# Projecting V ahead of the norm chain, and one FFN tile's projection inside the weight stage

## The chip, the cores and the metric

The program runs on all 8 NeuronCores of one Trainium2 chip. Each core computes one batch element with the same code and the same weights. There is no traffic between cores. The metric is the device time of the slowest core in microseconds (us).

## The reference, cut to what matters

```
x: (8, 2048, 2048); 16 heads of width 128
a = LayerNorm(x)
q, k, v = a @ W_Q[h] + b_Q, a @ W_K[h] + b_K, a @ W_V[h] + b_V
z = softmax(causal(q k^T / sqrt(128))) v          for each head
x = x + LayerNorm(z @ W_O + b_O)                  W_O summed over heads
bw = where(W >= 0, 1, -1) * mean|W| by row        W: (2048, 2048)
x = x + LayerNorm(LayerNorm(x) @ bw^T + bias)
```

## The kernel before

Every instruction is put by hand into one of five queues (sync, tensor, vector, scalar, gpsimd) by `p.op`. Each queue is executed in the order in which it was written, and what one engine needs of another is a wait on a counter. So where a Python function is called sets the place of its work in all queues at once.

The work of a core has four stages.

1. **LayerNorm 1** (`emit_A_head`, `emit_A_tail`, L235 to L282, loop at L385). The normalised tokens are transposed into `arena_a`, 2048 x 2048 in bf16. The projections of head 0 are done here, four slices of 512 tokens each, as the tokens become ready.
2. **Sixteen heads** (loop at L450). A projection is `emit_w_mms(h, wi)`: 64 matmuls of 128x512 into four PSUM banks, and then four VectorE instructions (L373) that add the bias and move the result to SBUF. `wi` is 0 for Q, 1 for K and 2 for V. Q and V use the banks of `psA` and `psB`, K those of `psD`, `psE` and `psC`. In the vector and tensor queues a head stands in this order: K projection; the norm chain of q (square on VectorE L462, four matmuls with a matrix of ones L471, four maxima L477, one more L483), the same for k, then two logarithms and an exponential on one element (L487 to L503), a matmul that spreads the number over the partitions (`pe_mb`, L507) and its copy to `mbias` (L512); the V projection (L518); the 16 transposes of V (L537) and their copy into `v_sb` (L543); then four groups of query tokens (scores L555, exp L569, causal mask on GpSimd L588 and L591, denominator L601, L606 and L610, scaling L620, product with V L637). The next head's Q projection is put into the tensor queue in the last group, ahead of the product with V (L630). Head 0 has its three projections behind it when the loop starts, so its V transposes stand right behind `pe_mb`.
3. **Weight stage** (`emit_bw_tile`, L398, called 16 times at L667). Each call loads 128 rows of the FFN weight into one of two buffers (`fwst`), takes the sum of absolute values (L411), the sign (L420) and the scaled weight (L423) on VectorE, transposes it on TensorE (L437) into `psD` and `psE`, and copies it to `arena_a` on VectorE (L443).
4. **Output loop** over 16 tiles of 128 tokens (L876). `emit_front_pe(i)` is the output projection: loads of x and z, 64 matmuls (L728) and 4 for the bias (L733) into `psA` and `psB`, two copies to `s1` on ScalarE (L744, L747), the statistics (L759, L762) and the factors (L221, L225, L769). `emit_front_chain(i)` adds the residual (L780) and normalises (L210, L787). `emit_back(i)` is the FFN product and the output. Tile i's projection stands ahead of the back part of tile i-1.

The buffers `xin` (x of a tile) and `s1` lie in memory that attention used and the weight stage does not. `x2` lies where the weight stage's first buffer lies.

Of the kernel before, what the change touches and what calls it, by code (L numbers as in the profile page):

```python
# [60 lines left out]
def build_program(SEQ, DM, H):  # L61
    assert SEQ == DM
    NCH = DM // 128
    NT = SEQ // 128
# [12 lines left out]
    p = Plan(nc)  # L77
# [91 lines left out]
    FWs = [p.sem(f"FW{i}") for i in range(2)]  # L169
# [134 lines left out]

    dv_mbias_d = {}
    dv_bw_evac_half = [0, 0]
# [4 lines left out]
    def emit_w_mms(h, wi, only_slice=None):  # L311
# [15 lines left out]
        for sq0, nq in slices:  # L327
            for c in range(NCH):
                wait = []
                if c == 0:  # L330
# [3 lines left out]
                    if sidx == 0:  # L334
                        prev_evac = dv_qkv_evac_d.get((h, 1), 0) if wi == 2 \
                            else dv_bank_free
                        wait += [("DV", dv_zevac.get(gidx - 1, 0)),
                                 ("DV", dv_mbias_prev),
                                 ("SC", sc_rinv_prev),
                                 ("DV", max(dv_bw_evac_half)),  # L340
                                 ("DV", prev_evac)]
                        if wi == 2:
                            wait.append(("DV", dv_mbias_d.get(h, 0)))
                    else:
                        wait += [("SC", max(psbuf_last_rd)),
                                 ("DV", dv_vch.get(h - 1, 0)),
                                 ("DV", dv_red_last)]
                for k in range(nq):
                    s = sq0 + k
# [100 lines left out]
    for h in range(H):  # L450
        if h > 0:
            emit_w_mms(h, 1)
        dv_mx = [0, 0]
        dv_red_all = {}
        for which, src_sb in ((0, qt_sb), (1, kt_sb)):
            if which == 0:
                w0 = [("DV", dv_qkv_evac_d[(h, 0)]), ("PE", pe_mb_prev),
                      ("PE", pe_bw_last)]
            else:
                w0 = [("PE", pe_norm_last),  # L460
                      ("DV", dv_qkv_evac_d[(h, 1)])]
            dv_sq = p.op("vector", lambda e, s=src_sb: e.tensor_mul(  # L462
                sqb, s[:], s[:]), wait=w0, inc="DV")
            for s in range(NSL):
# [4 lines left out]
                else:  # L469
# [38 lines left out]
            psC[:, 0:1], oner_sb[:], nm_bf[:], start=True, stop=True),  # L508
            wait=[("DV", dv_nm), ("DV", dv_qkv_evac_d[(h, 1)]),
                  ("SC", sc_rinv_prev)], inc="PE")  # L510
# [3 lines left out]
        dv_mbias_prev = dv_mbias  # L514
        dv_mbias_d[h] = dv_mbias

        if h > 0:
            emit_w_mms(h, 2)  # L518
        dv_qkv_evac = [dv_qkv_evac_d[(h, wi)] for wi in range(3)]
        dv_qkv_all = max(dv_qkv_evac)  # L520
        if h + 1 < H:
            for wi in range(3):
                emit_w_load(h + 1, wi)
        wo_start = max(0, H - 4)
        if h >= wo_start:
            win = H - wo_start
            per = (H + win - 1) // win
            hh0 = (h - wo_start) * per
            for hh in range(hh0, min(hh0 + per, H)):
                p.op("gpsimd", lambda e, hh=hh: e.dma_start(  # L530
                    Bz[:, hh * DM:(hh + 1) * DM], wo_h.ap()[hh]),
                    inc="WO", incn=16)

# [127 lines left out]

    B0_PE = p.cnt("PE")
    B0_DV = p.cnt("DV")
    B0_SC = p.cnt("SC")
    B0_GP = p.cnt("GP")
    for t in range(NT):
        emit_bw_tile(t)  # L667

    B_PE = p.cnt("PE")
# [103 lines left out]
    def emit_front_chain(i):  # L773
        nonlocal sc_r3_prev, dv_ln3_prev
        par = i % 2
        wait = [("SC", sc_r2[i]), (XCs[par], xc_t[i])]
        if i == 0:
            wait += [(FWs[0], fw_tot[0]), (FWs[1], fw_tot[1]), ("DV", B_DV)]
        p.drain("vector")
# [12 lines left out]
    def emit_back(i):  # L792
# [51 lines left out]
        for ci, (d, srcp) in enumerate(s2_copies):  # L844
# [29 lines left out]
            wait=[("DV", gp_x3[i])], inc="OUT0", incn=16)  # L874

    for i in range(NT):  # L876
        emit_front_pe(i)
        if i > 0:
            emit_back(i - 1)
        emit_front_chain(i)  # L880
# [53 lines left out]
```

How the kernel before makes its waits and increments, by code:

```python
        def thunk(e, fn=fn, wait=wait, inc=inc, incn=incn, lowp=lowp):  # L43
            for (s, v) in wait:
                e.wait_ge(sems[s][0], v)
            if lowp is not None:
                with nc.allow_low_precision(reason=lowp):
                    ins = fn(e)
            else:
                ins = fn(e)
            if inc is not None:
                ins.then_inc(sems[inc][0], incn)
```

## Time and profile before

| what | value |
|---|---|
| device time, median of 3 runs | 2764.18 us (2762.92 to 2764.88) |
| profiled execution, device time | 2761.78 us |
| its span, first to last instruction, slowest core (core 6) | 2760.0 us |
| spans of the other cores | 2756.1 to 2758.8 us |
| mean granted TensorE clock, all cores | 0.847 to 0.851 of full speed |
| busy: TensorE, VectorE, ScalarE, GpSimd | 71%, 36%, 20%, 9% |
| chain that ended last: TensorE, VectorE, ScalarE, issue | 52%, 18%, 10%, 9% |

The span is the time on which the profile's views are drawn; 1.8 us lie around it. A share of busy time is a mean over four stages with different limits, so a stage is judged by its own stretch of the span. PEclk is the TensorE clock granted, as a fraction of 2.4 GHz: 1.00 is the upper level and 0.50 the lower (1.2 GHz). A row of the timeline reads: start, length, engine, line, operation, what is written and read, how often, and in brackets the idle time ahead of it with what ended it. A length of several instructions is that of the whole row.

### The profile page before, as it was taken

Reading aid. Unit: us, or ns where it says so; the run is one execution under the profiler, and the core shown is the slowest. Engines: PE = TensorE matmul, PEld = TensorE weight load, DVE = VectorE, ACT = ScalarE, POOL = GpSimd, SP = SyncE. Lnnn points to the kernel's source line nnn. Section 1 sums busy time; section 2 is a strip of 40 time slices with the busy share of each in tenths; the row PEclk is TensorE's granted clock in tenths of the full one; section 3 lists DMA queues with packets and bytes.
Section 4 is the critical chain, followed back from the end, with each engine's and each line's share of the span. In section 5 each row is a group of like instructions: output and inputs, shape, how many; then the busy total and the mean of one; then the engine's idle time right before and its main releaser. Section 6 shows DMA issues by size and latency. Waiting matters only on the chain.

```text
span 2760.0 us, 27071 instructions; the slowest of 8 cores (2756.1 to 2760.0 us)
## 1 busy us (share of the span) xinstructions
PE 1956.9 (71%) x8336; PEld 824.0 (30%) x8336; DVE 990.8 (36%) x1760; ACT 554.9 (20%) x737; POOL 239.9 (9%) x558
## 2 busy tenths in 40 slices
PE   2568677677786777867777687677228778778774
PEld 1323232232332323323223232232123333333331
DVE  3532323232322322233223323232772453353353
ACT  1213213123032130321312303123001111111110
POOL 1001101011010110110101111111000000000000
PEclk9679889898898888978989889898559889889887
DMA  6321021120210211102112241320530321221210
GB/s 147 121 24 24 12 27 15 19 29 6 25 24 12 27 14 18 24 12 27 14 19 25 41 56 19 45 37 9 182 107 24 76 77 39 77 77 50 65 54 31
DMA packets 178473, 119.31 MB, mean 43 GB/s; under 512 B 168100, under 2 KB 168100, under 8 KB 170148
## 3 DMA queue, kind: packets, MB, share of 16 engines
q0 software_dynamic: 107200, 75.51, 15.7%
q1 hardware_dynamic: 71140, 42.07, 6.1%
q8 instruction: 78, 1.28, 0.2%
q14 instruction: 55, 0.45, 0.1%
HBM read 125.97 MB, written 25.17 MB: 55 GB/s over the span
## 4 chain that ended last, share of the span: by engine, by line
PE 52%; DVE 18%; ACT 10%; issue 9%; DVEq 5%; POOL 3%; DMA 2%; ACTq 1%; POOLq 0%; SPq 0%
PE psA L359 9%; PE psB L359 9%; PE psE L637 7%; ACT ptil L569 5%; PE psC L824 5%; DVEq L58 4%; PE psC L359 4%; PE psC L601 3%; DVE st L210 3%; PE psD L824 2%; PE psE L824 2%; POOL ptil L591 2%; PE psD L359 2%; PE psE L359 2%; DMA c<-x 2%
## 5 line engine op out<-in xcount | busy, mean ns | idle before, releaser
L620 DVE TENSOR_TENSOR ptil<-ptil,c 128x512 bf16<-128x512 bf16 x640 | 220.3, 418 | 509.0 <-ACT c L610 509.0
L359 PE MATMUL psA<-arena_a,wbuf 128*128 128x512 bf16 x1024 | 323.7, 405 | 10.3 <-DVE mbias L512 6.0
L359 PE MATMUL psB<-arena_a,wbuf 128*128 128x512 bf16 x1024 | 320.1, 401 | 3.2 <-ACT arena_a L276 3.2
L569 ACT ACTIVATE ptil<-psA,mbias 128x1024 bf16<-128x1024 f32 x160 | 178.3, 1114 | 492.7 <-PE psA L555 409.1
L637 PE MATMUL psE<-ptil,v 128*128 128x512 bf16 x640 | 193.5, 399 | 51.3 <-DVE ptil L620 51.3
L601 PE MATMUL psC<-ptil,onem_sb 128*128 128x512 bf16 x640 | 188.8, 411 | 49.9 <-POOL ptil L588 23.2
L824 PE MATMUL psC<-arena_a,c 128*128 128x512 bf16 x512 | 167.2, 411 | 57.5 <-DVE c L811 57.5
L591 POOL TENSOR_TENSOR ptil<-ptil,tri_sb 128x128 bf16<-128x128 bf16 x256 | 109.3, 427 | 1087.9 <-ACT ptil L569 1087.8
L569 ACT ACTIVATE ptil<-psB,mbias 128x1024 bf16<-128x1024 f32 x160 | 177.1, 1107 | 0.2 <-issue 0.2
L555 PE MATMUL psA<-qt,kt 128*128 128x512 bf16 x320 | 112.6, 438 | 75.7 <-ACT ptil L569 48.5
L359 PE MATMUL psC<-arena_a,wbuf 128*128 128x512 bf16 x544 | 157.2, 379 | 4.5 <-DVE qt L373 4.5
L210 DVE BATCH_NORM_STATS2 st<-wbuf 128x6 f32<-128x512 f32 x64 | 39.6, 681 | 313.9 <-ACT wbuf L847 313.9
L359 PEld LDWEIGHTS psB<-arena_a,wbuf 128*128 128x128 bf16 x1024 | 105.5, 103 | 139.7 <-issue 33.4
L359 PEld LDWEIGHTS psA<-arena_a,wbuf 128*128 128x128 bf16 x1024 | 104.3, 102 | 143.2 <-issue 37.7
L555 PE MATMUL psB<-qt,kt 128*128 128x512 bf16 x320 | 113.1, 440 | 22.9 <-ACT ptil L569 22.8
L487 ACT ACTIVATE srow<-srow 1x1 f32<-1x1 f32 x16 | 3.2, 202 | 608.7 <-DVE srow L483 608.7
L637 PEld LDWEIGHTS psE<-ptil,v 128*128 128x128 bf16 x640 | 62.2, 97 | 187.1 <-issue 152.4
L601 PEld LDWEIGHTS psC<-ptil,onem_sb 128*128 128x128 bf16 x640 | 64.8, 101 | 178.2 <-issue 132.0
L471 PE MATMUL psA<-c,onem_sb 128*128 128x512 bf16 x64 | 30.0, 551 | 119.3 <-DVE c L462 119.3
L373 DVE TENSOR_SCALAR ptil<-psA,bqkvT_sb 128x512 bf16<-128x512 f32 x32 | 22.6, 747 | 250.9 <-PE psB L359 245.5
L359 PE MATMUL psD<-arena_a,wbuf 128*128 128x512 bf16 x240 | 90.9, 379 | 21.7 <-DVE c L653 21.7
L824 PE MATMUL psD<-arena_a,c 128*128 128x512 bf16 x256 | 105.4, 412 | 0.0
(121 smaller groups left out, 2269.0 us busy)
## 6 DMA issues: line engine op xcount, KB each, us to landing
c<-fw POOLq DMA_DIRECT2D x16, 1024.0 KB, 5.1
ptil<-x SPq DMA_DIRECT2D x16, 1024.0 KB, 8.2
out<-wbuf POOLq DMA_DIRECT2D x16, 1024.0 KB, 5.5
wbuf<-wq POOLq DMA_DIRECT2D x16, 512.0 KB, 6.6
wbuf<-wk POOLq DMA_DIRECT2D x16, 512.0 KB, 6.7
c<-x SPq DMA_DIRECT2D x8, 1024.0 KB, 5.3
wbuf<-wv POOLq DMA_DIRECT2D x16, 512.0 KB, 6.5
zs<-c SPq DMA_DIRECT2D x64, 128.0 KB, 1.9
```

The source lines that it names most:

```text
L58: self.plans[eng].append(lambda e: e.drain())
L210: p.op("vector", lambda e, g=g, a=src_ap, pr=par: e.bn_stats(st6[pr][:, 6 * g:6 * g + 6], a[:, STW * g:STW * (g + 1)]), wait=w)
L359: e.matmul(banks[bidx], wslot[sl][:, c * 128:(c + 1) * 128], ln1t3[:, c, s * SLW:(s + 1) * SLW], start=(c == 0), stop=(c == NCH - 1)),
L373: e.tensor_scalar(d[:, s * SLW:(s + 1) * SLW], banks[bidx], bqkvT_sb[:, wi * H + h:wi * H + h + 1], None, ALU.add), wait=[("PE", pe_mm)],
L471: pe_norm_last = p.op("tensor", lambda e, s=s, hb=hb: e.matmul([psA[:, 0:SLW], psA[:, 512:512 + SLW], psB[:, 0:SLW], psB[:, 512:512 + SLW] ...
L555: pe_sc[j] = p.op("tensor", lambda e, j=j, g=g, hb=hb: e.matmul(schalf[hb], kt_sb[:, j * 128:(j + 1) * 128], qt_sb[:, g * GQ:(g + 1) * GQ] ...
L569: t_exp = p.op("scalar", lambda e, buf=buf, dst=dst: e.activation(dst, buf, AF.Exp, bias=mbias[:, 0:1], scale=C_ATTN), wait=wait, inc="SC")
L591: gp_mask_j[j] = p.op("gpsimd", lambda e, j=j, r=r: e.tensor_tensor(ptil[:, j * GQ + r * 128:j * GQ + (r + 1) * 128], ptil[:, j * GQ + r * ...
L601: pe_den = p.op("tensor", lambda e, j=j, chunks=chunks: e.matmul(psC[:, 512:512 + GQ], onem_sb[:], pslot[j], start=(j == 0), stop=(j == ch ...
L620: dv_norm[j] = p.op("vector", lambda e, j=j, g=g: e.tensor_tensor(pslot[j], pslot[j], rbc[g % 2], ALU.mult), wait=wait, inc="DV")
L637: pe_av = p.op("tensor", lambda e, j=j, chunks=chunks: e.matmul(psE[:, 0:GQ], v_sb[:, j * 128:(j + 1) * 128], pslot[j], start=(j == 0), st ...
L824: p.op("tensor", lambda e, c=c, s=s: e.matmul(ffnb[s], ln3t[:, c * 128:(c + 1) * 128], bwt3[:, c, s * 512:s * 512 + PSW], start=(c == 0), ...
```

## The change

Two pieces of work are moved, and the waits that go with them.

- For heads 1 to 15 the V projection (`emit_w_mms(h, 2)`) stands right behind the K projection, ahead of the norm chain. It now waits for the copies of Q out of the same banks. The squaring of q waits for the V copies. The loads for the next head and the `wo` loads are written earlier in the text; in the gpsimd queue nothing stands between the two places.
- The weight stage is written behind the definitions of the output loop, and after its fifth tile (t == 4) `emit_front_pe(0)` is called, in all queues: the loads of x and z for token tile 0, its 68 matmuls, the two copies, the statistics and the factors. The output loop then starts with `emit_front_chain(0)`. `emit_front_chain(0)` waits for all loads of the weight stage.

```diff
@@ -302,7 +302,6 @@
     dv_qkv_evac_d = {}
     pe_w_done_d = {}
 
-    dv_mbias_d = {}
     dv_bw_evac_half = [0, 0]
     dv_bw_evac_last = 0
     dv_fw_free = {}
@@ -332,19 +331,17 @@
                     if only_slice is not None:
                         wait.append(("DV", dv_qkv_evac_d.get((h, wi), 0)))
                     if sidx == 0:
-                        prev_evac = dv_qkv_evac_d.get((h, 1), 0) if wi == 2 \
-                            else dv_bank_free
                         wait += [("DV", dv_zevac.get(gidx - 1, 0)),
                                  ("DV", dv_mbias_prev),
                                  ("SC", sc_rinv_prev),
                                  ("DV", max(dv_bw_evac_half)),
-                                 ("DV", prev_evac)]
-                        if wi == 2:
-                            wait.append(("DV", dv_mbias_d.get(h, 0)))
+                                 ("DV", dv_qkv_evac_d.get((h, 0), dv_bank_free))]
                     else:
                         wait += [("SC", max(psbuf_last_rd)),
                                  ("DV", dv_vch.get(h - 1, 0)),
                                  ("DV", dv_red_last)]
+                        if wi == 2:
+                            wait.append(("DV", dv_qkv_evac_d.get((h, 0), 0)))
                 for k in range(nq):
                     s = sq0 + k
                     w = list(wait) if k == 0 else []
@@ -450,15 +447,30 @@
     for h in range(H):
         if h > 0:
             emit_w_mms(h, 1)
+            emit_w_mms(h, 2)
+        dv_qkv_evac = [dv_qkv_evac_d[(h, wi)] for wi in range(3)]
+        dv_qkv_all = max(dv_qkv_evac)
+        if h + 1 < H:
+            for wi in range(3):
+                emit_w_load(h + 1, wi)
+        wo_start = max(0, H - 4)
+        if h >= wo_start:
+            win = H - wo_start
+            per = (H + win - 1) // win
+            hh0 = (h - wo_start) * per
+            for hh in range(hh0, min(hh0 + per, H)):
+                p.op("gpsimd", lambda e, hh=hh: e.dma_start(
+                    Bz[:, hh * DM:(hh + 1) * DM], wo_h.ap()[hh]),
+                    inc="WO", incn=16)
+
         dv_mx = [0, 0]
         dv_red_all = {}
         for which, src_sb in ((0, qt_sb), (1, kt_sb)):
             if which == 0:
-                w0 = [("DV", dv_qkv_evac_d[(h, 0)]), ("PE", pe_mb_prev),
+                w0 = [("DV", dv_qkv_evac[2]), ("PE", pe_mb_prev),
                       ("PE", pe_bw_last)]
             else:
-                w0 = [("PE", pe_norm_last),
-                      ("DV", dv_qkv_evac_d[(h, 1)])]
+                w0 = [("PE", pe_norm_last)]
             dv_sq = p.op("vector", lambda e, s=src_sb: e.tensor_mul(
                 sqb, s[:], s[:]), wait=w0, inc="DV")
             for s in range(NSL):
@@ -506,30 +518,12 @@
             "softmax is shift-invariant so the value need not be exact")
         pe_mb = p.op("tensor", lambda e: e.matmul(
             psC[:, 0:1], oner_sb[:], nm_bf[:], start=True, stop=True),
-            wait=[("DV", dv_nm), ("DV", dv_qkv_evac_d[(h, 1)]),
+            wait=[("DV", dv_nm), ("DV", dv_qkv_evac[1]),
                   ("SC", sc_rinv_prev)], inc="PE")
         pe_mb_prev = pe_mb
         dv_mbias = p.op("vector", lambda e: e.tensor_copy(
             mbias[:], psC[:, 0:1]), wait=[("PE", pe_mb)], inc="DV")
         dv_mbias_prev = dv_mbias
-        dv_mbias_d[h] = dv_mbias
-
-        if h > 0:
-            emit_w_mms(h, 2)
-        dv_qkv_evac = [dv_qkv_evac_d[(h, wi)] for wi in range(3)]
-        dv_qkv_all = max(dv_qkv_evac)
-        if h + 1 < H:
-            for wi in range(3):
-                emit_w_load(h + 1, wi)
-        wo_start = max(0, H - 4)
-        if h >= wo_start:
-            win = H - wo_start
-            per = (H + win - 1) // win
-            hh0 = (h - wo_start) * per
-            for hh in range(hh0, min(hh0 + per, H)):
-                p.op("gpsimd", lambda e, hh=hh: e.dma_start(
-                    Bz[:, hh * DM:(hh + 1) * DM], wo_h.ap()[hh]),
-                    inc="WO", incn=16)
 
         wait = [("DV", dv_qkv_all), ("DV", dv_mx[1])]
         for t in range(NT):
@@ -659,13 +653,6 @@
                 wait=[("DV", dv_zevac[gidx])], inc=ZWs[zpar], incn=16)
             gidx += 1
 
-    B0_PE = p.cnt("PE")
-    B0_DV = p.cnt("DV")
-    B0_SC = p.cnt("SC")
-    B0_GP = p.cnt("GP")
-    for t in range(NT):
-        emit_bw_tile(t)
-
     B_PE = p.cnt("PE")
     B_DV = p.cnt("DV")
     B_SC = p.cnt("SC")
@@ -775,6 +762,9 @@
         par = i % 2
         wait = [("SC", sc_r2[i]), (XCs[par], xc_t[i])]
         if i == 0:
+            wait += [(FWs[0], fw_tot2[0]), (FWs[1], fw_tot2[1]),
+                     ("DV", B_DV)]
+        if i == 0:
             wait += [(FWs[0], fw_tot[0]), (FWs[1], fw_tot[1]), ("DV", B_DV)]
         p.drain("vector")
         gp_x2[i] = p.op("vector", lambda e, par=par: e.scalar_tensor_tensor(
@@ -873,8 +863,25 @@
             out_h.ap()[i * 128:(i + 1) * 128, :], x3buf),
             wait=[("DV", gp_x3[i])], inc="OUT0", incn=16)
 
+    B0_PE = p.cnt("PE")
+    B0_DV = p.cnt("DV")
+    B0_SC = p.cnt("SC")
+    B0_GP = p.cnt("GP")
+    for t in range(NT):
+        emit_bw_tile(t)
+        if t == 4 and NT >= 12:
+            emit_front_pe(0)
+
+    B_PE = p.cnt("PE")
+    B_DV = p.cnt("DV")
+    B_SC = p.cnt("SC")
+    B_GP = p.cnt("GP")
+    fw_tot2 = [p.cnt("FW0"), p.cnt("FW1")]
+
+    pre = 1 if NT >= 12 else 0
     for i in range(NT):
-        emit_front_pe(i)
+        if i >= pre:
+            emit_front_pe(i)
         if i > 0:
             emit_back(i - 1)
         emit_front_chain(i)
```

## Rows read from the trace of the kernel before

**Rows 1.** Windows by stage: core, from:to, length, busy of each engine (count), PEclk, DMA.

```profile
273.80:1886.40 1612.60, 1205.25 (x4807) 473.96 (x4807) 489.24 (x1032) 370.64 (x437) 188.77 (x448) 0.87 0.19 23
...
1938.50:2071.00 132.50, 30.59 (x259) 26.50 (x260) 101.97 (x113) 0.00 (x0) 7.43 (x14) 0.51 0.42 136
```

**Rows 2.** Waits: who waited for whom, us in total, times, longest.

```profile
PE psA L471 <- DVE c L462: 119.3, 32, 4.4
```

**Rows 3.** Timeline of head 3, K copies to the copy of V.

```profile
498.69 0.75 DVE L373 TENSOR_SCALAR kt<-psD,bqkvT_sb 128x512 bf16<-128x512 f32 x1 [14.65 <-PE psC L359]
...
501.34 1.22 DVE L462 TENSOR_TENSOR c<-qt 128x2048 bf16<-128x2048 bf16 x1
...
513.48 0.16 DVE L512 COPY mbias<-psC 128x1 f32<-128x1 f32 x1 [0.62 <-PE psC L507]
...
513.76 1.01 PE L359 MATMUL psA<-arena_a,wbuf 128*128 128x512 bf16 x2 [0.39 <-DVE mbias L512]
...
530.00 1.41 DVE L373 TENSOR_SCALAR ptil<-psA,bqkvT_sb 128x512 bf16<-128x512 f32 x2 [16.36 <-PE psB L359]
...
534.14 1.23 DVE L543 COPY v<-psA 128x2048 bf16<-128x2048 bf16 x1 [1.42 <-PE psA L537]
```

**Rows 4.** Windows in head 3: Q projection and AV, K projection, start of V projection.

```profile
465.00:484.00 19.00, 18.02 (x83) 7.88 (x81) 8.83 (x21) 1.18 (x2) 2.31 (x3) 1.00 0.38 37
484.60:498.40 13.80, 13.79 (x64) 6.24 (x64) 0.00 (x0) 0.00 (x0) 0.00 (x0) 1.00 0.22 27
...
513.70:518.20 4.50, 4.44 (x11) 1.68 (x12) 0.00 (x0) 0.00 (x0) 0.00 (x0) 0.51 0.00 0
```

**Rows 5.** Timeline of VectorE in head 0, and the Q copies of head 1.

```profile
182.98 1.22 DVE L462 TENSOR_TENSOR c<-qt 128x2048 bf16<-128x2048 bf16 x1
...
194.36 0.16 DVE L512 COPY mbias<-psC 128x1 f32<-128x1 f32 x1 [0.52 <-PE psC L507]
196.30 1.23 DVE L543 COPY v<-psA 128x2048 bf16<-128x2048 bf16 x1 [1.78 <-PE psA L537]
...
254.94 1.41 DVE L373 TENSOR_SCALAR qt<-psA,bqkvT_sb 128x512 bf16<-128x512 f32 x2 [6.90 <-PE psB L359]
```

**Rows 6.** Timeline of VectorE, first and last of heads 1 to 15.

```profile
273.80 0.75 DVE L373 TENSOR_SCALAR kt<-psD,bqkvT_sb 128x512 bf16<-128x512 f32 x1 [14.65 <-PE psC L359]
...
308.88 1.23 DVE L543 COPY v<-psA 128x2048 bf16<-128x2048 bf16 x1 [1.42 <-PE psA L537]
...
367.70 1.41 DVE L373 TENSOR_SCALAR qt<-psA,bqkvT_sb 128x512 bf16<-128x512 f32 x2 [6.90 <-PE psB L359]
...
1773.24 1.23 DVE L543 COPY v<-psA 128x2048 bf16<-128x2048 bf16 x1 [1.42 <-PE psA L537]
...
1831.28 1.41 DVE L373 TENSOR_SCALAR qt<-psA,bqkvT_sb 128x512 bf16<-128x512 f32 x2 [7.18 <-PE psB L359]
...
1850.15 0.75 DVE L373 TENSOR_SCALAR kt<-psD,bqkvT_sb 128x512 bf16<-128x512 f32 x1 [14.65 <-PE psC L359]
...
1886.38 1.23 DVE L543 COPY v<-psA 128x2048 bf16<-128x2048 bf16 x1 [2.23 <-PE psA L537]
```

**Rows 7.** Timeline, last weight tile and the first two output projections.

```profile
2070.04 1.06 PE L728 MATMUL psA<-arena_b,qt 128*128 128x512 bf16 x2
2070.36 0.69 DVE L443 COPY arena_a<-psE 128x1024 bf16<-128x1024 bf16 x1 [0.16 <-PE psE L437]
...
2087.06 2.47 DVE L759 BATCH_NORM_STATS2 st<-c 128x6 f32<-128x512 f32 x4 [16.01 <-ACT c L744]
...
2088.23 1.00 PE L728 MATMUL psA<-arena_b,kt 128*128 128x512 bf16 x2 [2.66 <-ACT c L747]
...
2090.69 0.16 DVE L769 TENSOR_TENSOR corr<-mv,rstd 128x1 f32<-128x1 f32 x1 [0.82 <-ACT rstd L225]
...
2105.06 1.01 ACT L744 COPY c<-psA 128x1024 f32<-128x1024 f32 x1 [7.50 <-PE psB L733]
```

**Rows 8.** DMA issues: bytes of each, median us from issue to landing.

```profile
wbuf<-wv POOLq DMA_DIRECT2D x16, 512.0 KB, 6.5
```

## Prediction

> **What bounds the kernel now.** I read the page first, then the windows by stage, the waits, and the timelines of one head and of the join between weight stage and output loop. By the windows [rows 1] heads 1 to 15 take 1612.6 us, and TensorE is busy for 1205 us of them; the rest is idle time. No engine fills that stage, so the chain through the engines counts. The waits name one place where TensorE stands still in every head: 119.3 us before the matmuls of the norm chain [rows 2]. The timeline of head 3 [rows 3] shows why. After the K projection VectorE copies K out (498.69), then squares q (501.34), and the small steps run one after another until `mbias` is written (513.48). Only then does the V projection start (513.76). Its result is copied at 530.00, transposed, and copied again at 534.14. TensorE's queue is in order, so V's matmuls, which need nothing of the norm chain, wait behind `pe_mb`. The clock belongs to the same picture [rows 4]: it is granted at 1.00 through Q projection, product with V and K projection, and is at 0.51 in the first 4.5 us of V, after the sparse norm chain.
>
> The weight stage is 132.5 us with VectorE busy for 102 and TensorE for 31 [rows 1]. VectorE and TensorE take turns in it.
>
> **Part one: V ahead of the norm chain, 15 heads.** I sum from the start of the K copies to the start of the copy into `v_sb`, since before and after these points the order stays.
>
> Before, in head 3 [rows 3]: K copies 2.65 (498.69 to 501.34), norm chain 12.14 (to 513.48), 0.28 to the first matmul of V, V projection 16.24 (to 530.00), V copies, transposes and waits 4.14 (to 534.14). Sum 35.45. The first head has 35.08 and the last 36.23 [rows 6]; over the 15 the mean is 35.22, with extremes 34.86 and 36.23.
>
> After:
> - V projection, straight behind K at the upper level: 64 matmuls in 13.80, as the window of the K projection shows [rows 4]. The K copies run on VectorE meanwhile and cost nothing, because the next thing that needs VectorE is the V copies 13.80 later. Were this cover missing they would cost their 2.65. The copies of Q already run beside matmuls at clock 1.00 [rows 4].
> - V copies, exposed: 2.65, four of the same instruction and shape.
> - Norm chain: 12.14 in head 3, 11.38 in head 0 (182.98 to 194.36) [rows 5]. It depends on when in it the clock falls. I take 11.8.
> - From `mbias` to the copy into `v_sb`: head 0 has exactly the new order, transposes right behind `pe_mb`, and shows 1.94 (194.36 to 196.30) [rows 5]. This holds the transposes at the lower level, and no V copy stands in between.
> - Sum 13.80 + 2.65 + 11.8 + 1.94 = 30.19.
>
> The gain is 35.22 - 30.19 = 5.03 a head, 75.5 us for 15. About half is that V no longer starts at the lower clock (16.24 against 13.80); the other half is that only one group of four copies is exposed instead of two, less the slower transposes.
>
> New waits: V waits for Q's copies, which ran during the product with V, long ago by then. Square of q waits for V's copies, but these stand ahead of it in its own queue. The loads keep their order in the gpsimd queue and wait for the same projections. The V weights are wanted some 15 us earlier; they were issued a head before and land in 6.5 us [rows 8]. All this costs nothing.
>
> Next late is the scores stage, which now always starts after a longer stretch at the lower clock. From the copy into `v_sb` to the next Q copies head 0 needs 58.64 (196.30 to 254.94) [rows 5]; head 1 needs 58.82 and head 14 58.04, the mean over 14 is 58.55 [rows 6]. So head 0, which has the new order, is no slower. I cost it at nothing, with half a microsecond a head to both sides, 7.5 in all. The norm chain's ends, 11.38 and 12.14, give 6 less or 5 more.
>
> The rule that speaks against the change is about long dense stretches. Here the clock stood at 1.00 from 465.0 to 498.4 [rows 4], and the mean clocks of the eight cores are equal to 0.004. The Trainium skill, "TensorE: Matmul & The Clock Gate", Part 1, says that a peak-current limiter takes a die to 13/16 of its clock once three of its cores run dense matmuls. By that, as an estimate from the page, V would take 17.0 instead of 13.80, the gain would be 1.8 a head, and the end near 2736. The rows show no such level in 33 us, so the sum goes by 13.80.
>
> **Part two: projection of tile 0 inside the weight stage.** It looks as if 68 matmuls were put where TensorE idles. But `emit_front_pe(0)` goes into all queues. In VectorE's queue the statistics of `s1` now stand ahead of the sixth weight tile, and they need the whole projection. So VectorE stands still during it, and the weight stage with it. The rows of the join give the price [rows 7]. From the end of the last weight copy (2070.36 + 0.69 = 2071.05) to the end of the factors (2090.69 + 0.16 = 2090.85) it is 19.8 us. This moves into the weight stage and delays its end by 19.8. At the end, the projection of tile 1 then starts right behind the last weight transposes, at 2070.04 + 19.8 = 2089.84, where it started at 2088.23 before. That is 1.6 later. Its length may be 15.8, as that of tile 0 that followed the transposes (the statistics at 2087.06 follow the first copy, 1.2 after the last matmul), or 16.8, as its own (2088.23 to 2105.06). That gives back up to 1.0. The projection in the weight stage may have more matmuls at the lower clock than before: 0 to 1.5. The sum lies between +0.6 and +3.1, and I take +1.3, nearer to the low end because both projections follow weight transposes, as the faster of the two did. The residual and LayerNorm of tile 0 run on VectorE during the projection of tile 1, before as after. The weight loads wait for `fwst`, and both buffers are full by the time that VectorE resumes; a load that was late would gain here, but none is seen to be.
>
> **Sum.** 2761.78 (the profiled execution, span 2760.0 and 1.8 around it) - 75.5 + 1.3 = 2687.6. The median of the runs is 2.4 above the profiled execution; I put the prediction between, at 2689.
>
> **The rivals.**
> - *Clock (the other side).* The unbroken run grows from 33 to 47 us, and TensorE's clock falls in it. Place: the V projection. At the lower level 64 matmuls take twice 13.80, which costs 13.8 against a gain of 5.03: 8.8 a head, 132 us, about 2894. It decides from the point at which 23 of the 64 run at the lower level. For it speaks the page's rule above, against it 33 us at 1.00. 3%. A partial form of it with the page's 13/16 is the 2736 above; I give it 3% more.
> - *The lower clock is carried into the scores stage.* Between the V projection and the second group TensorE has only short bursts. If the upper level comes back later than in head 0, 1 to 2 us a head are lost, 15 to 30 in all: 2704 to 2719. For it speaks that the new order has nothing dense after the norm chain, against it head 0. 8%.
> - *The projection of tile 0 is hidden after all.* If VectorE were not held, its 15.8 us and the statistics would vanish beside the weight stage: about 17 less, 2672. Against it stands the in-order queue. 4%.
> - *Part one does nothing*, because V waits for something that comes only with the chain, say the previous head's copy or a buffer of weights. The waits in the code name nothing of the kind. About 2763. 2%.
>
> **How the numbers follow.** The forecast (faster by 2.7%) has 80%, with a range of its own of 2680 to 2699 from the 7.5 and the 6 above and the bounds of part two. To hold 8 in 10 over all cases I take 2676 to 2706. This reaches into the third and second rival and leaves out the rest. A measurement of this kernel tells 0.2% (5.5 us) from no change. Faster: forecast, second and third rival and the partial clock case, 95%. Same: 2%. Slower: 3%.
>
> **What the profile after would show.** K and V as 128 matmuls in about 27.6 us at clock 1.00, with the K copies beside them; K copies to `v_sb` copy near 30.2; transposes behind `pe_mb` with nothing between; 58 to 59 us from there to the next Q copies; a pause of VectorE of about 16 us in the weight stage, which is near 152 us long; and one projection at the join. A K copy that lies after V's last matmul, a clock under 1.00 in V, or a scores stage over 60 us would make the prediction wrong.

## The result, and the profile after

The changed kernel takes 2687.35 us (median of 9 runs, 2685.42 to 2701.96), against 2764.18 for the kernel before in the same comparison. In some executions of every kernel the cores of one die are granted a lower clock and take longer; the medians and ratios of this document leave these out. The ratio is 0.9728, 95% interval 0.9712 to 0.9745: 2.7% faster. The prediction was 2689 with a range of 2676 to 2706. The profiled execution took 2685.89, with a span of 2684.1 on core 3, so the span is 75.9 shorter than before.

First the page: its first line, the busy times, and the projection groups that write `psA` and `psB` (mean ns of one ahead of the second bar, idle time behind it).

```profile
span 2684.1 us, 27075 instructions; the slowest of 8 cores (2678.5 to 2684.1 us)
...
PE 1926.6 (72%) x8336; PEld 825.9 (31%) x8336; DVE 991.4 (37%) x1760; ACT 554.7 (21%) x737; POOL 239.3 (9%) x558
...
L356 PE MATMUL psA<-arena_a,wbuf 128*128 128x512 bf16 x1024 | 304.2, 384 | 4.3 <-ACT arena_a L276 3.1
L356 PE MATMUL psB<-arena_a,wbuf 128*128 128x512 bf16 x1024 | 303.8, 384 | 2.8 <-ACT arena_a L276 2.8
```

The number of instructions on TensorE is the same, 8336, but it is busy 30 us less. The two projection groups are where it fell: `psA` from 323.7 to 304.2 us and `psB` from 320.1 to 303.8, in the mean from 405 and 401 ns to 384. (These are more than 30 together, because the busy times of groups overlap.) These groups hold Q and V. V no longer starts at the lower clock.

The timeline of head 3 answers to [rows 3].

```profile
487.34 0.75 DVE L370 TENSOR_SCALAR kt<-psD,bqkvT_sb 128x512 bf16<-128x512 f32 x1 [14.65 <-PE psC L356]
...
501.16 1.41 DVE L370 TENSOR_SCALAR ptil<-psA,bqkvT_sb 128x512 bf16<-128x512 f32 x2 [11.09 <-PE psB L356]
...
504.06 1.22 DVE L474 TENSOR_TENSOR c<-qt 128x2048 bf16<-128x2048 bf16 x1 [0.17 <-DVE ptil L370]
...
515.52 0.16 PE L519 MATMUL psC<-nm_bf,oner_sb 1*128 1x1 bf16 x1 [3.07 <-DVE nm_bf L515]
...
515.75 1.86 PE L531 MATMUL psA<-eye_sb,ptil 128*128 128x128 bf16 x16
515.78 0.16 DVE L524 COPY mbias<-psC 128x1 f32<-128x1 f32 x1 [0.62 <-PE psC L519]
517.72 1.23 DVE L537 COPY v<-psA 128x2048 bf16<-128x2048 bf16 x1 [1.78 <-PE psA L531]
```

K copies at 487.34, V copies at 501.16: 13.82 apart. Square of q at 504.06, `mbias` at 515.78, copy into `v_sb` at 517.72. From the first to the last it is 30.38, where it was 35.45 [rows 3]. `pe_mb` (L519) is followed by the transposes (L531) with nothing between, as in head 0 before [rows 5].

The windows of the same head answer to [rows 4]: product with V and K projection, V projection, norm chain, transposes, and last the K and V projections as one stretch.

```profile
469.00:487.00 18.00, 16.56 (x78) 7.44 (x76) 2.90 (x5) 0.00 (x0) 1.06 (x1) 1.00 0.35 37
487.20:501.10 13.90, 13.85 (x65) 6.08 (x62) 2.73 (x4) 0.00 (x0) 1.14 (x1) 1.00 0.40 38
501.20:515.60 14.40, 3.81 (x9) 0.94 (x9) 10.62 (x18) 0.70 (x3) 0.00 (x0) 0.58 0.00 1
515.70:517.70 2.00, 1.86 (x16) 1.63 (x16) 0.16 (x1) 0.00 (x0) 0.00 (x0) 0.50 0.00 0
473.26:501.04 27.78, 27.78 (x128) 12.50 (x128) 2.73 (x4) 0.00 (x0) 1.14 (x1) 1.00 0.32 33
```

The clock is 1.00 through K and V, and falls only in the norm chain (0.58). The K copies (2.73 us of VectorE, four instructions) lie in the window of the V projection and don't disturb it: its 13.90 us hold all 64 matmuls (the 65th of the count is K's last). K and V together are 128 matmuls in 27.78 us, where the prediction had 27.6. The transposes run at 0.50.

Last the weight stage, which answers to [rows 7]: its first reduction, the moved projection of tile 0 with the statistics and factors on VectorE, the next weight tile, and the projection of tile 1 at the join.

```profile
1860.36 2.28 DVE L408 TENSOR_REDUCE asum<-c 128x1 f32<-128x2048 f32 x1
...
1900.74 1.06 PE L715 MATMUL psA<-arena_b,qt 128*128 128x512 bf16 x2
1901.06 0.69 DVE L440 COPY arena_a<-psE 128x1024 bf16<-128x1024 bf16 x1 [0.16 <-PE psE L434]
...
1918.26 2.47 DVE L746 BATCH_NORM_STATS2 st<-c 128x6 f32<-128x512 f32 x4 [16.52 <-ACT c L731]
...
1921.89 0.16 DVE L756 TENSOR_TENSOR corr<-mv,rstd 128x1 f32<-128x1 f32 x1 [0.82 <-ACT rstd L225]
1921.99 2.29 DVE L408 TENSOR_REDUCE asum<-c 128x1 f32<-128x2048 f32 x1
...
2012.60 1.06 PE L715 MATMUL psA<-arena_b,kt 128*128 128x512 bf16 x2
...
2029.21 1.01 ACT L731 COPY c<-psA 128x1024 f32<-128x1024 f32 x1 [8.84 <-PE psB L720]
```

VectorE stands still for 16.52 us (in brackets at 1918.26) and takes up the sixth weight tile at 1921.99, right behind the factors (L756). From the end of the last weight copy ahead of it (1901.06 + 0.69) to the end of the factors (1921.89 + 0.16) it is 20.3 us. The stage takes 152.2 us from its first reduction to the projection behind it (2012.60), where the prediction had 152.

For the sums I take, over heads 1 to 15, the means of the distances that the timelines give on the slowest core of each run, in us:

| kernel | K copies to `v_sb` copy | square of q to `mbias` | `mbias` to `v_sb` copy | `v_sb` copy to next Q copies | head period |
|---|---|---|---|---|---|
| before | 35.22 | 11.80 | 20.78 | 58.57 | 112.68 |
| changed | 30.35 | 11.68 | 1.95 | 58.27 | 107.50 |
| filler matmuls on before | 32.92 | 11.49 | 18.79 | 58.30 | 110.13 |
| square waits for Q | 30.11 | 11.71 | 1.94 | 58.52 | 107.51 |
| woven chain | 20.33 | 15.69 | 2.00 | 58.13 | 97.35 |
| filler matmuls on changed | 29.21 | 11.37 | 1.13 | 57.71 | 105.81 |
| woven, spread, filler | 19.82 | 15.68 | 1.50 | 57.89 | 96.58 |

(The fourth column is over heads 1 to 14, the last is the distance of the `v_sb` copies of heads 1 and 15 over 14. The second column holds part of the V projection in the woven kernels.)

The slowest core is one of eight, and for small differences all eight tell more. Their means for the fourth column and the head period are 58.53 and 112.65 before, 58.16 and 107.40 in the changed kernel, and 58.29 and 107.28 where the square waits for Q.

### The profile page after: what moved, and what is told of

Its sections match the earlier page's. It is cut to its first block, busy times and chain, and to the rows that moved or that the text cites. A ratio compares the mean times of both kernels' runs of the same rounds, so it can differ in the third digit from the quotient of the medians.

```text
span 2684.1 us, 27075 instructions; the slowest of 8 cores (2678.5 to 2684.1 us)
## 1 busy us (share of the span) xinstructions
PE 1926.6 (72%) x8336; PEld 825.9 (31%) x8336; DVE 991.4 (37%) x1760; ACT 554.7 (21%) x737; POOL 239.3 (9%) x558
## 4 chain that ended last, share of the span: by engine, by line
PE 53%; DVE 17%; ACT 10%; issue 9%; DVEq 5%; POOL 3%; DMA 2%; ACTq 1%; POOLq 0%
PE psA L356 8%; PE psB L356 8%; PE psE L631 7%; ACT ptil L563 5%; DVEq L58 5%; PE psC L814 5%; PE psC L356 4%; PE psC L595 3%; DVE st L210 3%; PE psD L814 2%; PE psE L814 2%; POOL ptil L585 2%; PE psD L356 2%; PE psE L356 2%; DMA c<-x 2%
## 5 line engine op out<-in xcount | busy, mean ns | idle before, releaser
L356 PE MATMUL psA<-arena_a,wbuf 128*128 128x512 bf16 x1024 | 304.2, 384 | 4.3 <-ACT arena_a L276 3.1
L356 PE MATMUL psB<-arena_a,wbuf 128*128 128x512 bf16 x1024 | 303.8, 384 | 2.8 <-ACT arena_a L276 2.8
L814 PE MATMUL psC<-arena_a,c 128*128 128x512 bf16 x512 | 167.2, 411 | 57.5 <-DVE c L801 57.5
L221 ACT ACTIVATE rstd<-mv,epsb_sb 128x1 f32<-128x1 f32 x64 | 18.9, 295 | 416.0 <-DVE mv L213 379.8
```

The source lines that it names most:

```text
L221: p.op("scalar", lambda e, pr=par: e.activation(rstd[pr][:], mv2[pr][:, 1:2], AF.Ln, bias=epsb_sb[:, 0:1], scale=1.0), wait=w)
L356: e.matmul(banks[bidx], wslot[sl][:, c * 128:(c + 1) * 128], ln1t3[:, c, s * SLW:(s + 1) * SLW], start=(c == 0), stop=(c == NCH - 1)),
L814: p.op("tensor", lambda e, c=c, s=s: e.matmul(ffnb[s], ln3t[:, c * 128:(c + 1) * 128], bwt3[:, c, s * 512:s * 512 + PSW], start=(c == 0), ...
```

## The experiments

Medians are of runs on the same chip in turn with the kernel before, whose median was 2764.5, 2763.5 and 2763.2 in the three sets. They are set beside 2687.35 of the changed kernel, which ran in a set of its own.

### Each part alone

V moved, tile 0 not:

```diff
-        if t == 4 and NT >= 12:
-            emit_front_pe(0)
...
-    pre = 1 if NT >= 12 else 0
+    pre = 0
```

> Only the V projection is moved; the projection of token tile 0 stays behind the weight stage. Theory (part one carries all, part two costs a little): 5.0 to 5.2 us a head, so 2685 to 2690 against 2765 before, and not slower than the kernel with both parts. Rival (part two hides the projection of tile 0 and brings some 15 us of the gain): about 2702.

Measured: 2684.96, ratio 0.9715 (0.9697 to 0.9734). Part one alone has all of the gain.

Tile 0 moved, V not:

```diff
+    for t in range(NT):
+        emit_bw_tile(t)
+        if t == 4 and NT >= 12:
+            emit_front_pe(0)
...
+    pre = 1 if NT >= 12 else 0
     for i in range(NT):
-        emit_front_pe(i)
+        if i >= pre:
+            emit_front_pe(i)
```

> Only the projection of token tile 0 is moved into the weight stage; the heads are as before. Theory (VectorE stands still for the projection, so the time only changes place): 0.6 to 3.1 us slower than before, 2765 to 2768. Rival (the projection is hidden beside the weight stage): 15 to 17 us faster, about 2749.

Measured: 2765.10, ratio 1.0009 (0.9995 to 1.0023). The rival that the projection is hidden, with its 15 us, is out. The cost itself is within what the runs can tell from nothing; the profile has it, since from the first reduction of the weight stage to the ScalarE copy of tile 1's projection it is 166.5 us before, 168.9 in the changed kernel (1860.36 to 2029.21 above), 167.2 with V alone and 169.3 with the tile alone. One core differs from another by up to 2 us in this distance; the means over all eight, in the same order, are 166.6, 168.8, 166.3 and 169.0. So moving the tile costs 2.5 with V moved and 2.4 without.

### What the gain of part one is made of

First the cover of the K copies is taken away. VectorE makes them only after V's last matmul.

```diff
+            if hold:
+                held_k.append((h, wi, banks, dst))
...
+            if held_k:
+                kh, kwi, kbanks, kdst = held_k.pop()
+                for k in range(4):
...
+                                        None, ALU.add), wait=[("PE", pe_mm)],
+                        inc="DV")
...
-            emit_w_mms(h, 1)
+            emit_w_mms(h, 1, hold=True)
             emit_w_mms(h, 2)
```

> The changed kernel, but VectorE copies K out only after the last matmul of V, ahead of the V copies, so that the cover of the K copies is gone. Theory: eight copies stand between the V projection and the norm chain instead of four, 2.65 us more a head, 40 us in all: 2727. Rival (the gain comes from the clock alone, copies don't count): 2687 to 2695.

Measured: 2727.90, ratio 0.9869 (0.9853 to 0.9884), so 40.6 us above the changed kernel, 2.70 a head. The clock stays at 1.00 through K and V, so it is the copies and not the clock that this run changes. In the timeline of one head the K copies now stand behind the V projection, and the square of q comes 5.53 after the first of them:

```profile
506.06 0.75 DVE L374 TENSOR_SCALAR kt<-psD,bqkvT_sb 128x512 bf16<-128x512 f32 x1 [28.47 <-PE psB L356]
...
511.59 1.23 DVE L490 TENSOR_TENSOR c<-qt 128x2048 bf16<-128x2048 bf16 x1 [0.17 <-DVE ptil L385]
```

In the changed kernel the square comes 2.90 after the first V copy, so the exposed copies count in full: 2.63 for four.

Then the clock, without moving V. Extra matmuls fill TensorE's idle time in the norm chain of the kernel before. They write to banks that nobody reads then: 18 to `psB` ahead of the norm matmuls of q, 14 and 12 to `psD` behind those of q and of k.

```diff
+            if h > 0 and which == 0:
+                for f in range(18):
+                    p.op("tensor", lambda e, f=f: e.matmul(
+                        psB[:, 512:512 + SLW], ln1t3[:, f % 16, 0:128],
+                        ln1t3[:, f % 16, 0:SLW], start=True, stop=True),
...
+            if h > 0:
+                for f in range((14, 12)[which]):
+                    p.op("tensor", lambda e, f=f: e.matmul(
+                        psD[:, 0:SLW], ln1t3[:, f, 0:128],
```

> The kernel before, with 44 extra matmuls a head (18 ahead of the norm matmuls of q, 14 behind them, 12 behind those of k) whose results nobody reads. They fill TensorE's idle time in the norm chain so that its clock stays up; the place of V is as before. Theory (about half of the gain of part one is the clock): V projection 13.8 us instead of 16.2, norm chain some 0.5 us shorter, 40 to 45 us less in all: 2720 to 2725. Rival (all of the gain is the hidden copies and waits): V projection still over 16 us or its gain lost to the extra matmuls, 2760 or more.

Measured: 2724.70, ratio 0.9858 (0.9844 to 0.9872), 40 us less than before with 660 matmuls more. The windows show a norm chain, a V projection and the transposes of one head:

```profile
490.00:504.40 14.40, 12.49 (x53) 4.96 (x52) 10.61 (x18) 0.70 (x3) 1.14 (x1) 1.00 0.38 37
505.10:519.00 13.90, 13.89 (x64) 6.24 (x64) 0.00 (x0) 0.00 (x0) 0.00 (x0) 1.00 0.01 1
522.20:524.10 1.90, 1.84 (x16) 1.58 (x16) 0.00 (x0) 0.00 (x0) 0.00 (x0) 0.50 0.00 0
```

The clock stays at 1.00 through the chain, and V takes its 64 matmuls in 13.9. So keeping the clock up, with no work moved, is worth 40 us where the change has 77. By the table 2.30 of the 2.55 us a head lie ahead of the `v_sb` copy, the rest in the scores stage. A small part of the 2.30 is a shorter norm chain (11.49 against 11.80), which the changed kernel has less of (11.68). The V copies between V projection and transposes are still exposed beside those of K, and that is the other half.

One term of the prediction was 0.25 short: the square of q starts 2.90 after the first V copy (504.06 - 501.16), not 2.65. In the changed kernel it waits for the copy just ahead of it in its own queue. It needs only the Q copies.

```diff
-                w0 = [("DV", dv_qkv_evac[2]), ("PE", pe_mb_prev),
+                w0 = [("DV", dv_qkv_evac[0]), ("PE", pe_mb_prev),
```

> The changed kernel, but the square of q waits for the copies of Q, which is what it reads, and not for the last copy of V, which stands just ahead of it in the same queue. In the changed kernel the square starts 2.90 us after the first V copy, before it started 2.65 after the first K copy. Theory (the wait on its own neighbour costs 0.25 us a head): 3.7 us less, 2683.6. Rival (it is the banks or the operand, not the wait): 2687.

Measured: 2686.43, ratio 0.9718 (0.9704 to 0.9731): 0.9 less than the changed kernel, where the theory had 3.7. Both are within what the runs can tell from nothing, so the traces must say. The wait did what the theory said. The first V copy and the square of q in one head:

```profile
502.04 1.41 DVE L370 TENSOR_SCALAR ptil<-psA,bqkvT_sb 128x512 bf16<-128x512 f32 x2 [11.09 <-PE psB L356]
...
504.68 1.22 DVE L474 TENSOR_TENSOR c<-qt 128x2048 bf16<-128x2048 bf16 x1
```

They are 2.64 apart, and the mean over the heads is 2.64 against 2.90. On the slowest core none of the 0.26 is left: the scores stage is 58.52 instead of 58.27, and the head period is the same to 0.01. Over all eight cores the stage gives back half, 58.29 against 58.16, and the head period is 0.12 shorter, which makes about 2 us in all. The theory was right on the wait; of the time about half comes out on the average core and nothing on the slowest.

### The lower clock in the scores stage

This asked for a test of how much the scores stage owes to the clock. Extra matmuls go into the changed kernel, around the norm matmuls and behind the V transposes.

```diff
+            if h > 0 and which == 0:
+                for f in range(19):
...
+            if h > 0:
+                for f in range((14, 12)[which]):
...
         pe_vtr = tgt
+        if h > 0:
+            for f in range(7):
```

> The changed kernel, with 52 extra matmuls a head whose results nobody reads: 19 ahead of the norm matmuls of q, 14 behind them, 12 behind those of k, 7 behind the V transposes. They keep the clock up through the norm chain and into the scores stage; no real work is moved. Theory (what the order of the changed kernel still pays is the lower clock): norm chain 0.2 us shorter, transposes to the V copy 0.8 shorter, scores stage 1 to 1.5 shorter (58.3 to about 57), 2.0 to 2.5 a head, 2687 - 30 to 37 = 2650 to 2657. Rival (the first group of scores waits for ScalarE and GpSimd anyway and the clock matters little there): 2670 to 2675. Other rival (so long a dense stretch lowers the clock): W stretches under 1.00, over 2687.

Measured: 2662.26, ratio 0.9631 (0.9617 to 0.9645), 25 us less than the changed kernel, between the two expectations. Windows of the scores stage of one head: the first and second four us, and the whole. First the changed kernel:

```profile
517.72:521.72 4.00, 1.86 (x4) 0.50 (x4) 1.23 (x1) 1.19 (x2) 0.00 (x0) 0.50 0.00 0
521.72:525.72 4.00, 2.97 (x7) 0.91 (x8) 0.00 (x0) 1.51 (x2) 2.39 (x7) 0.50 0.00 0
...
517.72:576.20 58.48, 46.16 (x170) 16.85 (x171) 17.06 (x45) 25.73 (x28) 10.72 (x29) 0.89 0.13 16
```

And the one with extra matmuls:

```profile
514.47:518.47 4.00, 2.43 (x11) 0.82 (x9) 1.22 (x1) 1.62 (x2) 0.36 (x1) 1.00 0.00 0
518.47:522.47 4.00, 2.92 (x8) 0.86 (x8) 0.00 (x0) 1.68 (x3) 2.04 (x7) 0.84 0.02 4
...
514.47:571.88 57.41, 45.17 (x177) 17.07 (x176) 17.07 (x44) 25.67 (x28) 10.74 (x29) 0.97 0.13 17
```

The clock is 1.00 and 0.84 where it was 0.50 and 0.50, and the whole is 57.41 against 58.48 in this head. But over the heads the mean falls only from 58.27 to 57.71. The larger part of the 25 us is ahead of the stage: 0.82 in the transposes and 0.31 in the chain. In the first 8 us TensorE is idle for a third of the time at either clock (busy 4.83 and 5.35 us), so there is other work in the first group of scores than TensorE's, and the clock helps it little. That this is ScalarE's and GpSimd's, as the expectation's rival had it, is argued; no run tests it.

### Part two: what holds VectorE

The part of `emit_front_pe` from the statistics on becomes a function of its own. For tile 0 it is called behind the weight stage; the matmuls stay in one block behind the fifth tile.

```diff
+    def emit_front_stats(i):
...
     for i in range(NT):
         if i >= pre:
             emit_front_pe(i)
+        emit_front_stats(i)
```

> The changed kernel, but the statistics and factors of token tile 0 stand behind the weight stage in VectorE's queue; matmuls and ScalarE copies stay behind the fifth weight tile. Theory (VectorE was held by the statistics): it now goes on with the sixth weight tile, until the transposes of that tile, which stand behind 15.5 us of matmuls in TensorE's queue, hold it; of the 15.5 us some 6 lie in TensorE's idle time and the statistics' 4 are hidden later: about 10 us less than the changed kernel, 2677. Rival (the join costs the same wherever VectorE's part stands): 2687.

Measured: 2675.08, ratio 0.9679 (0.9666 to 0.9693), 12 us less than the changed kernel. VectorE now goes on with the sixth tile and is stopped one step later:

```profile
1907.79 1.35 DVE L420 TENSOR_SCALAR v<-c,twoal,negal 128x2048 bf16<-128x2048 f32 x1
...
1919.93 0.62 PE L434 MATMUL psD<-eye_sb,v 128*128 128x128 bf16 x8
...
1920.66 0.69 DVE L440 COPY arena_a<-psD 128x1024 bf16<-128x1024 bf16 x1 [11.52 <-PE psD L434]
```

The scaled weight is ready at 1907.79 + 1.35, but its transposes run only at 1919.93, behind the block of matmuls, and the copy had waited 11.52.

Then the 64 matmuls are spread, 8 behind each of tiles 4 to 11.

```diff
-        if t == 4 and NT >= 12:
-            emit_front_pe(0)
+        if t >= 4 and t < 12:
+            emit_front_pe(0, t - 4)
...
+        hhs = range(H) if part is None else range(2 * part, 2 * part + 2)
```

> As the kernel with the late statistics, but the 64 matmuls of token tile 0 are spread, 8 behind each of the weight tiles 4 to 11, so that each piece (3.4 us at the lower clock) fits into TensorE's 6.4 us of idle time. Theory: the projection of tile 0 is hidden, 18 to 20 us less than the changed kernel, 2668. Rival (TensorE's place in the weight stage is not free, each piece delays the next transposes): 2680 or more.

Measured: 2665.10, ratio 0.9641 (0.9626 to 0.9656), 22 us less than the changed kernel and 20 less than the one with V alone. The eight matmuls of one piece end well before the next transposes:

```profile
1910.64 1.06 PE L721 MATMUL psA<-arena_b,qt 128*128 128x512 bf16 x2
...
1911.49 0.66 PE L721 MATMUL psB<-arena_b,qt 128*128 128x512 bf16 x2
...
1911.99 0.59 PE L721 MATMUL psA<-arena_b,qt 128*128 128x512 bf16 x2
...
1912.42 0.59 PE L721 MATMUL psB<-arena_b,qt 128*128 128x512 bf16 x2
...
1917.23 1.01 PE L434 MATMUL psD<-eye_sb,v 128*128 128x128 bf16 x8 [4.21 <-DVE v L420]
```

From the first reduction of the weight stage to the copy of tile 1's projection it is 148.3 us (1861.91 to 2010.16), where the changed kernel has 168.9.

### A version that beats both

The norm chain is work that VectorE and ScalarE can do beside matmuls, if its own eight matmuls have a place in TensorE's queue. They are put into the V projection, those of q behind 20 of V's 64 and those of k behind 44, and write to the banks that the K copies have left free.

```diff
             for c in range(NCH):
+                if weave and c in (5, 11):
+                    emit_norm(h, 0 if c == 5 else 1)
...
-                    [psA[:, 0:SLW], psA[:, 512:512 + SLW], psB[:, 0:SLW],
-                     psB[:, 512:512 + SLW]][hb], onem_sb[:],
+                banksN[s], onem_sb[:],
```

> The changed kernel, with the norm chain woven into the V projection: the norm matmuls of q stand behind 20 of the 64 matmuls of V, those of k behind 44, and they use the banks that K has left. Theory (the chain is short work of VectorE and ScalarE that only needs a place beside matmuls): all of its 11.8 us a head but the 8 norm matmuls (1.7) is hidden, and the transposes are at the upper clock: 10 to 11 us a head, 2687 - 150 to 165 = 2522 to 2537. Rival (the chain then holds V's matmuls in the in-order queue): each of the two norm points waits 1 to 3 us, and 2550 to 2590 comes out. Other rival (the longer dense stretch lowers the clock): V projection over 15.5 us.

Measured: 2534.94, ratio 0.917 (0.9156 to 0.9184). The timeline of one head:

```profile
467.51 0.75 DVE L372 TENSOR_SCALAR kt<-psD,bqkvT_sb 128x512 bf16<-128x512 f32 x1 [14.65 <-PE psC L358]
...
470.15 1.22 DVE L465 TENSOR_TENSOR c<-qt 128x2048 bf16<-128x2048 bf16 x1
...
477.79 0.38 PE L471 MATMUL psD<-c,onem_sb 128*128 128x512 bf16 x1
...
482.02 0.14 DVE L506 TENSOR_SCALAR nm_bf<-srow 1x1 bf16<-1x1 f32 x1 [0.49 <-ACT srow L501]
...
483.06 0.17 PE L513 MATMUL psC<-nm_bf,oner_sb 1*128 1x1 bf16 x1
483.24 1.41 DVE L372 TENSOR_SCALAR ptil<-psA,bqkvT_sb 128x512 bf16<-128x512 f32 x2 [1.08 <-PE psC L513]
...
487.90 1.23 DVE L555 COPY v<-psA 128x2048 bf16<-128x2048 bf16 x1 [1.87 <-PE psA L549]
```

K copies at 467.51, the square of q right behind them, the norm matmuls of k at 477.79 among those of V. The number for `mbias` is ready at 482.02 + 0.14, one us ahead of V's end; `pe_mb` at 483.06 and the V copies at 483.24 follow at once. From K copies to `v_sb` copy it is 20.4. The window of V with the eight norm matmuls:

```profile
466.40:483.20 16.80, 16.69 (x76) 7.34 (x76) 10.57 (x18) 0.70 (x3) 1.14 (x1) 1.00 0.34 32
```

The clock is 1.00 throughout this window. From the K copies to `pe_mb` it is 15.55 (467.51 to 483.06). The V projection alone is 13.81, and eight more matmuls at its 0.216 each are 1.73, together 15.54: neither of the two norm points held V.

Woven and spread together:

> The woven norm chain and the spread projection of token tile 0 together. Theory (they lie in different stages and add): 2535 for the woven kernel less the 21 us that the spread kernel had against the changed one, 2514. Rival (they don't add, since the weight stage's start depends on the last head's clock): 2520 or more.

Measured: 2512.84, ratio 0.9114 (0.9081 to 0.9147); the interval is wide because one of the five executions took 2542.08. The woven kernel less the gain of the spread one would be 2534.94 - 22.25 = 2512.7. So they add, as closely as these runs can tell. The rival's 2520 or more lies above four of the five executions.

With 13 extra matmuls beside the V copies and 7 behind the transposes as well:

> The woven and spread kernel with 20 extra matmuls a head whose results nobody reads: 13 beside the V copies, 7 behind the transposes, so that the clock is still up when the scores start. Theory (the scores stage is shorter by what its first group loses at the lower clock): transposes 0.5 us and scores stage 1 to 1.5 us shorter, 15 heads, 22 to 30 us less than the woven and spread kernel, 2484 to 2492. Rival (no effect, or the clock falls in the first group all the same): 2514.

Measured: 2502.93, ratio 0.9054 (0.9042 to 0.9066), 10 us less, where 22 to 30 had been expected. It is the fastest kernel of the study. Against the woven kernel the table gives 0.5 a head in the transposes and 0.2 in the scores stage; the 1 to 1.5 of the expectation for the scores stage isn't there, as in the other filler run.

## Why the prediction was right, step by step

**V projection at the upper clock, K copies hidden.** 13.80 forecast, 13.81 measured as the mean distance from K copies to V copies. Right, and both halves are shown apart: the clock by the filler run (40 us), the cover by the run that takes it away (41 us). The prediction called the clock "about half", which these bear out; they add up to a little more than the 77.

**V copies exposed, 2.65.** It is 2.90, as the square of q now waits for its neighbour in the queue. Mis-sized by 0.25 a head, 3.7 in all. The prediction had this wait among those that cost nothing, since the V copies stand ahead of the square in its own queue. The wait is the cause of the 0.25, as the run without it shows, though taking it away gained only about half of it on the average core and nothing on the slowest.

**Norm chain 11.8, `mbias` to copy 1.94.** Measured 11.68 and 1.95. For the 1.94 head 0 of the kernel before was the model of the new order, and a good one. The 11.8 was a choice between its 11.38 and head 3's 12.14, and it is what the heads of the kernel before have in the mean.

**Sum of part one.** 30.19 forecast, 30.35 measured, so 73.0 us in place of 75.5.

**Scores stage, costed at nothing.** On the slowest cores it became 0.30 shorter a head, and 1.3 in head 0 (58.64 to 57.36): about 5.5 us that the sum hadn't, inside its bound of 7.5. (The mean before is 58.57, not the 58.55 of the prediction.) The 1.3 is luck. Head 0 takes 57.35 to 58.64 over the eight cores of the kernel before, and 57.31 to 58.53 in the changed one; the core that the prediction read happened to have the longest. So this one row was a weak ground for costing the stage at nothing. Over all eight cores head 0 went from 57.79 to 57.52, and heads 1 to 14 from 58.53 to 58.16.

Windows show two places in the stage that bear on this: its first 4 us and 4 us some 38 us in, in head 3 of the kernel before, and the same late place in head 1 of the changed kernel.

```profile
534.14:538.14 4.00, 1.86 (x4) 0.50 (x4) 1.23 (x1) 1.20 (x2) 0.00 (x0) 0.63 0.00 0
...
572.14:576.14 4.00, 3.54 (x10) 1.17 (x9) 0.00 (x0) 3.64 (x4) 0.78 (x3) 0.58 0.00 0
...
341.26:345.26 4.00, 3.24 (x15) 1.50 (x16) 0.00 (x0) 3.27 (x4) 1.57 (x5) 1.00 0.01 4
```

The start of the stage had little to lose: before, its first 4 us are at 0.63 and the next at 0.50, and in the changed kernel both are at 0.50. Later the clock falls a second time in some heads and not in others. Where it does (mean clock under 0.97 from 34 to 46 us into the stage), the stage takes 58.9 us in the mean, in both kernels; where it doesn't, 58.23 before and 58.05 in the changed kernel. Before, 53 of the 112 stages of heads 1 to 14 on eight cores have it, in the changed kernel 16. That is over half of the 0.37. Why it comes in fewer heads no run shows; it stays open.

**Part two.** +1.3 forecast, with bounds of 0.6 and 3.1. From the first reduction to the copy of tile 1's projection the changed kernel needs 2.3 more. The terms: 20.3 for the pause with statistics against 19.8, as the projection of tile 0 had more matmuls at the lower clock (its first to the copy 16.34 against 15.84, with a mean clock of 0.72 against 0.85 in its first 4 us). The projection of tile 1 starts 2.5 later against 1.6; 0.5 of the difference is the pause, and 0.4 lies in the other weight tiles, without a cause that a run shows. It takes 16.6, near the 16.8 of its own before, and not 15.8. So the step "nearer to the low end" chose the wrong row for its length. That the place of this work in the queues is what holds the stage is shown by the two runs that move it: 12 us for the statistics alone, 22 with the matmuls spread.

**Sum.** 78.2 us gained up to the first reduction of the weight stage (1938.52 to 1860.36), 2.3 lost behind it, 75.9 in the span. The forecast had 75.5 and 1.3. The loss in the copies (3.7) and in part two (1.0) and the gain in the scores stage (5.5) have opposite signs, so that the sum comes out within 2 us (75.9 against 74.2) is luck; the terms are good to some 5 us.

**The clock rival.** In no profiled execution did the clock fall in a long dense stretch: 1.00 from 469 to 501 in the changed kernel, and 1.00 from the Q projection to the end of V, some 46 us, in heads 1 to 15 on all eight cores of every kernel that has V behind K, those with filler matmuls and the woven ones too. The Trainium skill, "TensorE: Matmul & The Clock Gate", Part 1, has a limiter at 13/16 when three cores of a die run dense matmuls. All eight cores do so here, and these windows don't show it: 64 matmuls in 13.8 us are at the full clock. The prediction took this rule as speaking for its first rival as well, a fall to the lower level; it speaks only for the partial form.

## What to carry to other kernels

In an in-order queue ask, of each long wait, which work behind it needs nothing of what is waited for; moving it ahead pays twice where it also keeps TensorE's clock up. A call that emits work for all engines moves all of them: matmuls put where TensorE idles gain nothing if the same call leaves VectorE waiting for them in its own queue. If the head of a loop already runs in the new order, as head 0 did here, its rows give the new prices directly, if they are read on all cores: here one core's head 0 was up to 1.3 us longer than another's in the same stage.

## What the runs showed of the hardware that was not expected

- Extra matmuls whose results nobody reads made three kernels faster: 660 of them brought 40 us on the kernel before, 780 brought 25 us on the changed one, and 300 brought 10 us on the woven and spread one.
- The upper clock in the first 8 us of the scores stage (1.00 and 0.84 against 0.50) shortened a stage of 58.3 us by only 0.6 on the slowest core and 0.45 over all eight (58.16 to 57.71).
- About 34 to 46 us into a scores stage the clock falls a second time in some heads and not in others, on the same core and with the same instructions. Stages with the fall are some 0.7 us longer (58.9 against 58.2 before).
- A VectorE instruction that waits for the one just ahead of it starts 0.17 us after that one's end (in brackets at 504.06), where without the wait it had started 0.08 us ahead of it (501.34 against 500.02 + 1.40 for the copies just ahead, in head 3 of the kernel before). Taken away in all 15 heads, it shortened the head period by 0.12 over all cores and by nothing on the slowest.
